# Row maxima's chain ahead of the normalisation, query rotation a quarter later, q's second component issued by ScalarE

## The reference

```python
# x: (8, 512, 256); 32 query heads in 8 groups of 4; head size 64; window 128
xn = layernorm(x)
q, k, v = xn @ Wq + bq, xn @ Wk + bk, xn @ Wv + bv       # k and v: 8 heads
q, k = rope(q) * D ** -0.25, rope(k) * D ** -0.25        # interleaved pairs (even, odd)
    # first = even * cos - odd * sin;  second = odd * cos + even * sin
scores = where(|i - j| <= 128, q @ k.T, -1e9)
probs = softmax(concat([scores, sinks]))[..., :-1]
s = (probs @ v) @ Wo + bo
g = silu(fp8_quantised(xn) @ W_ffn.T + b_ffn)
out = x + s * g
```

## Time and profile before

| | |
|---|---|
| median of 3 runs | 2094.28 us (2089.43 to 2124.69) |
| profiled execution | 2088.92 us; span of its instructions 2087.2 us |
| PE busy | 1823.7 us (87%) |
| VectorE / ScalarE / POOL busy | 1304.4 (62%) / 727.5 (35%) / 1018.1 (49%) |
| mean granted PE clock | 0.896 of full speed |
| chain that ended last | PE 54%, DMA 10%, issue 9%, POOL 8%, VectorE 6%, SyncE's queue 6%, ScalarE 3% |
| steps | one of 64 takes some 28 to 36 us |

### The profile page before, as it was taken

How to read it: one execution, slowest core, us unless ns; L and a number is a source line. 1 busy time by engine, 2 the same in 40 slices (tenths; PEclk the granted TensorE clock), 3 DMA queues, 4 the chain that set the end, 5 groups by cost and what they waited for, 6 DMA issues and landing times.

```text
span 2087.2 us, 33771 instructions
## 1 busy us (share of the span) xinstructions
PE 1823.7 (87%) x11139; PEld 1603.5 (77%) x11139; DVE 1304.4 (62%) x4156; ACT 727.5 (35%) x1509; POOL 1018.1 (49%) x1019
## 2 busy tenths in 40 slices
PE   2379999999989899989989999899998989999998
PEld 1168888888878787778878888787887878878887
DVE  7646666656756666666666666665665666665564
ACT  2123333333433333333333333333343333333332
POOL 4335445545644554564464554554454554555451
PEclk8578998989999899998899889998899988999899
DMA  4442442443354343435235244344334434234441
GB/s 156 96 82 44 87 70 52 92 72 71 53 94 71 67 77 64 78 64 92 51 68 97 49 77 70 56 87 77 57 62 84 75 71 77 51 71 75 77 74 25
DMA packets 80957, 151.92 MB, mean 73 GB/s; under 512 B 12944, under 2 KB 30096, under 8 KB 76688
## 3 DMA queue, kind: packets, MB, share of 16 engines
q1 hardware_dynamic: 80784, 149.76, 38.8%
HBM read 18.64 MB, written 4.19 MB: 11 GB/s over the span
## 4 chain that ended last, share of the span: by engine, by line
PE 54%; DMA 10%; issue 9%; POOL 8%; DVE 6%; SPq 6%; ACT 3%; DVEq 0%; POOLq 0%
PE pv_bank L1142 16%; DMA qT_full<-q_second_hi 9%; PE ring L1103 8%; PE ring L1050 7%; PE score L1126 6%; PE score L1128 6%; PE acc L1165 5%; DVE junk L858 2%; PE ring L1059 2%; PE ring L1152 2%; SPq L369 2%; SPq L381 1%; POOL stage L544 1%; DMA qT_high<-turned_rows 1%; POOL q_second L500 1%
## 5 line engine op out<-in xcount | busy, mean ns | idle before, releaser
L858 DVE CUSTOM_DVE_ANT_0 junk<-ring,mask 128x384 bf16<-128x384 f32 (+1 forms) x1024 | 488.6, 485 | 573.0 <-PE ring L1103 564.7
L1142 PEld LDWEIGHTS pv_bank<-v,stage 128*128 128x128 f32 x5120 | 741.8, 206 | 26.5 <-issue 8.2
L1142 PE MATMUL pv_bank<-v,stage 128*128 128x65 f32 x5120 | 738.5, 278 | 1.0 <-ACT stage L623 0.5
L544 POOL TENSOR_SCALAR_AFFINE_SELECT stage<-stage 128x512 f32<-128x512 f32 x384 | 251.4, 670 | 714.0 <-ACT stage L623 713.9
L1103 PE MATMUL ring<-kT_high,qT_full 128*128 128x384 f32 (+1 forms) x1024 | 411.9, 403 | 83.7 <-DVE row_max L858 45.9
L623 ACT ACTIVATE stage<-score 128x512 f32<-128x512 f32 x640 | 356.4, 594 | 367.6 <-PE score L1128 366.5
L1126 PE MATMUL score<-qT_full,kT_high 128*128 128x512 f32 x640 | 290.9, 455 | 33.2 <-ACT stage L623 15.4
L1103 PEld LDWEIGHTS ring<-kT_high,qT_full 128*128 128x128 f32 x1024 | 212.6, 208 | 133.4 <-DVE row_max L858 78.6
L1128 PE MATMUL score<-qT_high,kT_low 66*128 66x512 f32 x640 | 274.4, 429 | 0.0
L664 ACT ACTIVATE oT_hi<-ring 128x256 fp32r<-128x256 f32 x256 | 98.4, 384 | 392.4 <-PE ring L1152 392.4
L485 POOL TENSOR_TENSOR q_first<-q_even,cos 128x512 f32<-128x512 f32 x64 | 82.3, 1286 | 255.8 <-DMA qT_full<-q_second_hi 255.8
(11 more groups left out here) (118 smaller groups left out, 2770.4 us busy)
## 6 DMA issues: line engine op xcount, KB each, us to landing
qT_high<-qT_full SPq DMA_DIRECT2D x64, 512.0 KB, 4.5
qT_full<-q_first SPq DMA_DIRECT2D x64, 256.0 KB, 4.2
qT_full<-q_first_hi SPq DMA_DIRECT2D x64, 256.0 KB, 5.6
qT_full<-q_second SPq DMA_DIRECT2D x64, 256.0 KB, 6.8
qT_full<-q_second_hi SPq DMA_DIRECT2D x64, 256.0 KB, 8.0
kT_high<-k_first_hi SPq DMA_DIRECT2D x128, 64.0 KB, 2.4
kT_high<-k_second_hi SPq DMA_DIRECT2D x128, 64.0 KB, 2.2
x_res<-in_x SPq DMA_DIRECT2D x11, 512.0 KB, 8.8
```

The lines of the kernel that those rows point to most:

```text
L544: nc.gpsimd.affine_select(out=pr, in_=pr, compare_op=ALU.is_ge, fill=0.0, base=0, pattern=[[0, GROUP], [sign, P]], channel_multiplier=-sign) \
L858: nc.vector.tensor_tensor_reduce(junk[:, h % 2, 0:cols], ring[h % 2][:, 0:cols], mask[:, m0:m0 + cols], 1.0, LOWEST, ALU.add, ALU.max, row ...
L1142: last = nc.tensor.matmul(pv[:, h, :], prob[:, q % 2 * 3 + n, h * P:(h + 1) * P], v[:, slot, k, :], start=(n == 0), stop=(n == len(BLOCKS[ ...
```

## The change

SyncE keeps only the first component in `queries_in`; the new `seconds_placed` issues the second component's two transfers from ScalarE, at the end of q=3, behind the same waits. The keys of k=6 are issued last in SyncE's step. POOL's `turn_even` goes from the end of q=0 to q=1 behind the cuts, with `turn_odd` behind it; `turn_rest` and `first_low` go to q=2 and `second_low` to q=3; `keys_low` of k=2 goes from q=2 to q=0. ScalarE's `first_high` goes from q=1 to q=2, `second_high` from q=1 to q=3 (behind the exponentials) and `keys_high` of k=2 from q=1 to q=0. VectorE's `negated` runs at the end of q=0 and q=2, ahead of `normalised`, and no more at the start of q=1 and q=3; in q=3 `o_low` goes behind the last maximum. PE's last row product of q=3 goes ahead of the last weighting. No arithmetic is added or left out.

```diff
--- before.py
+++ after.py
@@ -372,15 +372,12 @@
 
             def queries_in(a):
 
-                parts = ((0, q_first, q_first_hi, s_first_lo, s_qT_first_in),
-                         (HALF, q_second, q_second_hi, s_second_lo, s_qT_second_in))
                 upto(sp, s_score_pe, NB * (a - 1))
-                for row, low, high, ready, done in parts:
-                    sp.wait_ge(ready, a + 1)
-                    upto(sp, done, Q_IN * a)
-                    sp.dma_start(qT_full[row:row + HALF, a % 2, :, :].bitcast(F32), low[:, :]).then_inc(done, 16)
-                    sp.dma_start(qT_full[D + row:D + row + HALF, a % 2, :, :].bitcast(F32), high[:, :]) \
-                        .then_inc(done, 16)
+                sp.wait_ge(s_first_lo, a + 1)
+                upto(sp, s_qT_first_in, Q_IN * a)
+                for row, part in ((0, q_first), (D, q_first_hi)):
+                    sp.dma_start(qT_full[row:row + HALF, a % 2, :, :].bitcast(F32), part[:, :]) \
+                        .then_inc(s_qT_first_in, 16)
 
             def highs_in(b):
 
@@ -412,12 +409,14 @@
                     rows_in(it, 1)
                 if k == 0 and n >= 1:
                     result(n - 1, 0)
-                if real(t) and t % QUAD == 0:
+                if real(t) and k == 2:
                     keys_in(t)
                 if real(it + 1):
                     rows_in(it + 1, 0)
                 if real(a):
                     queries_in(a)
+                if real(t) and k == 6:
+                    keys_in(t)
                 if k == 0 and n >= 1:
                     result(n - 1, 1)
                 if it == 0:
@@ -555,22 +554,22 @@
                         rstd_of((it + 2) * TILES + q + 2)
                     if (k, q) == (1, 2) and 0 <= n < BATCH - 1:
                         rstd_of(n + BATCH)
-                    if q == 1 and real(a):
-                        turn_odd(a)
-                    if q == 3 and k == 6 and new_keys:
+                    if (k, q) == (6, 3) and new_keys:
                         keys_low(quad)
                     if real(it):
                         cut(it, q)
-                    if q == 0 and real(a):
+                    if q == 1 and real(a):
                         turn_even(a)
-                    if q == 1 and real(a):
+                        turn_odd(a)
+                    if q == 2 and real(a):
                         turn_rest(a)
                         first_low(a)
-                        second_low(a)
                     if (k, q) in ((2, 0), (6, 2)) and new_keys:
                         keys_sum(quad)
-                    if (k, q) == (2, 2) and new_keys:
+                    if (k, q) == (2, 0) and new_keys:
                         keys_low(quad)
+                    if q == 3 and real(a):
+                        second_low(a)
                     if k == 0 and n >= 1 and q in (1, 3):
                         finish(n - 1, q // 2)
 
@@ -643,6 +642,15 @@
                 act.wait_ge(s_rope, 6 * a + 6)
                 nc.scalar.activation(q_second_hi[:, :].bitcast(F32R), q_second[:, :], ACT.Copy) \
                     .then_inc(s_second_hi, 1)
+
+            def seconds_placed(a):
+
+                upto(act, s_score_pe, NB * (a - 1))
+                act.wait_ge(s_second_lo, a + 1)
+                upto(act, s_qT_second_in, Q_IN * a)
+                for row, part in ((HALF, q_second), (D + HALF, q_second_hi)):
+                    nc.scalar.dma_start(qT_full[row:row + HALF, a % 2, :, :].bitcast(F32), part[:, :]) \
+                        .then_inc(s_qT_second_in, 16)
 
             def keys_high(quad):
                 act.wait_ge(s_k_summed, 2 * quad + 2)
@@ -680,6 +688,8 @@
                         exps(it, q, 1)
                     if q == 0 and real(a):
                         odd_out(a)
+                    if q == 3 and real(a):
+                        second_high(a)
                     if other is not None and other[0] == "x":
                         x_high(other[1], 0)
                         x_high(other[1], 1)
@@ -694,10 +704,11 @@
                         max_rows(b, 0)
                     if real(back(it, q, 2)[0]):
                         o_high(*back(it, q, 2))
-                    if q == 1 and real(a):
+                    if q == 2 and real(a):
                         first_high(a)
-                        second_high(a)
-                    if (k, q) in ((2, 1), (6, 2)) and quad < BATCH * QUADS:
+                    if q == 3 and real(a):
+                        seconds_placed(a)
+                    if (k, q) in ((2, 0), (6, 2)) and quad < BATCH * QUADS:
                         keys_high(quad)
                     if it < 0 and fill + FIRST_CHUNKS < N_CHUNKS:
                         chunk_high(fill + FIRST_CHUNKS)
@@ -963,10 +974,6 @@
                     fill = (it + 2) * TILES + q
                     other = chunk_at(n, k, q)
                     r, tile = back(it + 1, q, 1)
-                    if q == 1 and real(it):
-                        negated(it, 1)
-                    if q == 3 and real(b):
-                        negated(b, 0)
                     if real(r):
                         maximum(r, tile, 0)
                     if other is not None:
@@ -979,10 +986,16 @@
                             x_low(other[1], 1)
                     beside(it, n, k, q)
                     for h in heads_of(tile)[1:]:
-                        if h == GROUP - 1 and real(back(it, q, 2)[0]):
+                        if h == GROUP - 1 and q < 3 and real(back(it, q, 2)[0]):
                             o_low(*back(it, q, 2))
                         if real(r):
                             maximum(r, tile, h)
+                    if q == 0 and real(it):
+                        negated(it, 1)
+                    if q == 2 and real(b):
+                        negated(b, 0)
+                    if q == 3 and real(back(it, q, 2)[0]):
+                        o_low(*back(it, q, 2))
                     if real(back(it, q, 1)[0]):
                         normalised(*back(it, q, 1))
                     if it < 0 and fill + 2 < BATCH:
@@ -1285,8 +1298,12 @@
                         row(1)
                         weighed(2)
                     heads_turn()
-                    weighed(3)
-                    row(3)
+                    if q == 3:
+                        row(3)
+                        weighed(3)
+                    else:
+                        weighed(3)
+                        row(3)
                     if real(c3[0]):
                         out_project(*c3)
```

## The result

The changed kernel takes 2139.22 us (median of 4 runs, 2118.75 to 2146.85) against 2092.39 for the kernel before in the same comparison: ratio 1.018, 95% interval 1.013 to 1.024. It is slower, by 1.8%, where I forecast 1975. Whether that is the forecast's "slower by over 2%" (0.09) or still "within it" (0.18), the interval doesn't tell. A ratio in this document is taken over fast executions alone and need not be the quotient of the medians beside it (1.022 here); in experiment 11 two of four executions, and in experiment 2 one of ten (2636 us), are left out of it. The profiled execution took 2135.1 us. TensorE's clock went down, not up: 0.877 over the span, before 0.896.

A forecast was written before the change was run, and what follows sets the result against it. TensorE was taken as busy nearly all the time, leaving its gaps and clock to be won. Terms -77 +36 +40 -20 -14 -21 +42 -105 sum to -119: 1975 us beside the median, range 1895 to 2090.

The forecast's parts named there:

- within it: Outcome class: measured time within about 2% of no change, 2052 to 2136 us; chance 0.18.
- Part 1: Maxima's chain, moved ahead of `normalised` with POOL idle beside it, takes 0.56 us; transposition's wait goes: -77 us.
- Part 4: `row(3)` ahead of `weighed(3)` in q=3: maximum runs beside the weighting, next query projection's wait goes: -20 us.
- Part 5: k=2: `second_high` and `keys_high` no longer ahead of the scores' exponentials; the scores' wait for ScalarE goes: -14 us.
- Rival (b): Pair 0's chain collides with POOL's products in every step, delaying `normalised` and q=3's weighting: 2183 us; chance 0.10.
- Parts 2 and 3: Later `normalised` makes the weighting wait, +36 us; pair 0's chain, at the end of q=2, meets POOL's products, +40.
- Part 2: Later `normalised` gives 0.45 us new wait at the weighting in 80 quarters q=1 and q=3: +36 us.
- Part 6: k=6 keys issued last, so SyncE no longer holds rows and queries; waits of 10.7 and 13.0 shrink: -21 us.
- Part 7: SyncE's queue delays the maxima's rows; 1.5 us wait before q=2 in k=4, 5, 7, 0.7 in k=0: +42 us.
- Part 8: ScalarE issues q's second component: costed at nothing, the four transfers taking 10.0 us; ends +77 and -38.
- Part 9: TensorE's clock: shorter waits leave 60 of the 165 us lost, -105; bounds nothing won, or 145.
- Rival (a): TensorE's gaps change place and its clock stays down; parts 1 to 7 give -14: 2080 us; chance 0.19.

The follow-up runs named there:

- experiment 11: Kernel before with only POOL's rotation a quarter later, ScalarE's compute that follows it, and SyncE's keys of k=6 last: 2069.57 us, ratio 0.976.
- experiment 2: Changed kernel with all four of q's transfers issued by SyncE again, no `seconds_placed`: 2094.31 us, ratio 0.999 to the kernel before.
- experiment 12: Best version (changed kernel, rows ahead of keys, pair 0 behind `normalised`, k=2 `keys_low` in q=1) with pair 1 behind `normalised` too: 1937.58 us, ratio 0.922.
- 8: Kernel before with only q's second component issued by ScalarE (`seconds_placed` and the shorter `queries_in`): 2153.06 us, ratio 1.025.
- 1: Changed kernel with SyncE issuing `rows_in(it, 1)` ahead of the six key transfers: 1989.78 us, ratio 0.945 to the kernel before.
- 4: Changed kernel with `rows_in(it, 1)` ahead of the keys and q's second component issued by SyncE: 2009.83 us, ratio 0.957 to the kernel before.
- 6: Changed kernel with rows ahead of keys, pair 0 behind `normalised`, and k=2 `keys_low` in q=1 behind the cuts: 1902.68 us, ratio 0.906, the fastest.
- 9: Fastest version (rows ahead of keys, pair 0 behind `normalised`, k=2 `keys_low` in q=1) with all four q transfers on SyncE: 1904.55 us, ratio 0.905.
- Experiment 7: Changed kernel with eight added products in k = 3, 4, 5 ahead of the score that opens q=2: 2070.38 us, ratio 0.987 to the kernel before.
- experiment 10: Kernel before with only VectorE's chain ahead of `normalised` and TensorE's `row(3)`, `weighed(3)` exchanged in q=3: 2185.66 us, ratio 1.037.

## Why the prediction was wrong

**Right.** Part 1 in its mechanism and size: 77.3 us at the transposition are gone, the chain takes 0.57 in every step but k = 2. Part 4: the maxima held the line of the projections for 22.1 us in 65 times, TensorE and its weight load together; now for 2.0 in two. Part 5: the 15.4 us went and k = 2 is 2.4 us shorter, not 4 or more. Rival (b) didn't happen: pair 0 mostly ends 0.3 or 1.35 us into q=3, and only in k = 6 at 3.7.

**Parts 2 and 3, right in sum by luck.** 76 us were forecast, 70.8 measured at the weighting. Part 2's short wait has the size (0.37 to 0.39 in q=1, forecast 0.45) but comes in 29 quarters and not 80: some 11 us in place of 36. The collisions take the other 60 in place of 40: pair 1 in k = 2 (a wait of 2.6 each time), pair 0 in k = 6 (2.9), and pair 0 in k = 0 and 2 (0.9 to 1.1).

**Part 6, half.** The scores' 10.7 us went; the row products' 13.0 are still 11.7.

**Part 7, the right wait at half its size.** I named the score that opens q=2 and the queue, and forecast 42 us; it measured 84.1 in 39 times. Most of the shortfall stands in steps that I had left out. Those that I named (k = 4, 5, 7 and 0) have 49 us: 2.6 a time in k = 4 and 5, 1.0 in k = 0, and in k = 7 a single wait of 0.3. The other 35 stand in k = 3 (2.9 a time, the longest) and k = 1 (1.6). In k = 4 and 5 I had 1.5 for the 2.6. The term for the work of q=1 was taken from the earlier trace rows as 5.84, and 0.45 put on top. The quarter's own work is 4.99 at full clock (experiment 12), or 5.60 with the wait of part 2 in it: the quarter in the row was not free of waiting itself (0.28 us before its transposition). That is 0.7 us a step. The rest is mostly the landing: I let q land 0.14 before q=1 as in the earlier trace rows, while it landed 0.2 to 0.45 into q=1 in k = 4, and 1.9 to 2.2 into it in k = 3 (four batch elements) and k = 0 (five), there behind the slower transfers issued in k = 2 and k = 7.

**Part 8, the step that failed outright.** "Costed at nothing", with four transfers of 10.0 us. I asked how much an issue costs ScalarE and whether two queues overlap. I didn't ask what SyncE would send in the gap that it no longer spends waiting. Experiments 2 and 8 price it: 45 us on the changed kernel, 2.5% on the kernel before. Experiments 1 and 4, and 6 and 9, show that ScalarE's own time costs nothing: where the landing is off the path, ScalarE may issue without loss. By the Trainium skill (DMA: Bandwidth & Descriptors, "Issuing engines are not separate DMA queues") a second issuing engine saves only the issuing time. The runs agree: where nothing comes between, the four take 9.9 us with one issuer and with two. The 11.5 us show that the order between the two issuers is a price of its own.

**Part 9, the step that decided the sign.** I gave 105 us back for the clock and took nothing won as the worst case, though I had written that waits of 1.5 and 2.4 us may not keep it. By the granted clock and the span, the kernel before lost 217 us (2087.2 at 0.896) and the changed one 262 (2133.3 at 0.877): 45 more lost in place of 105 won, 150 us of a miss of 164. With 3.2 us of wait the clock was 0.50 through the whole next quarter, 4.9 us lost behind one wait: dearer than the wait. Experiment 7 puts some 69 us on this in k = 3 to 5. The bound should have allowed a loss, since part 7 itself put waits in k = 4 and 5 of a length that might not keep the clock. Rival (a) had the right picture, gaps that change place and a clock that stays down, but took TensorE's gaps as a sum of -14; by the rows for TensorE's matmuls that I had priced it is +44 (77.3 + 15.4 + 10.7 + 13.0 + 6.3 = 122.7 for the transposition, the scores and the row products' issue before; 84.1 + 70.8 + 11.7 = 166.6 after), and its gaps of all kinds grew by 26 between the first step and the last; the clock was free to fall further.

**What stays open.** The length of a wait alone doesn't decide what the clock does behind it. In k = 4 of the changed kernel waits of 1.9 to 3.2 us were all followed by a q=2 at 0.50 to 0.54. In k = 1 one of 1.9 was followed by 1.00 and one of 2.6 by 0.82, and in k = 5 one of 2.7 by 1.00. What else decides it, no experiment separates. Why two of SyncE's six issues take over 1 us in the step shown was not looked into either. The shares by part depend on the order in which they are undone, as each shifts where the others meet.

## What to carry to other kernels

When a wait is removed, take the next bound's slack from a quarter with no wait in it, and price the longest wait that remains rather than their sum: one of 3 us cost more in clock than in itself. Before giving a transfer to a second issuing engine, write down what the first will send in its place, and let what is needed soonest go first in a queue: exchanging two calls was worth 149 us here. Where two engines slow each other when they meet, a quarter that becomes shorter moves the later meetings, so a small speed-up can be a loss: 35 us here (experiment 12).

## What the hardware did that I had not expected

- Added products made the kernel 69 us faster (experiment 7). A wait of 3.23 us was followed by 10.7 us at clock 0.50, one of 0.86 behind busy fillers by 5.8 at 1.00. A quarter with a wait of 0.64 in it (experiment 6) kept 1.00, the same quarter with one of 1.02 (experiment 12) fell to 0.70.
- Two transfers issued by ScalarE landed behind what SyncE had issued in the meantime: 10.3 to 11.7 us for q's four in 27 of the 32 steps of k = 0, 2, 6 and 7, in place of some 9.9. Where SyncE issued nothing between, 9.9 as on one issuer: neither gain nor loss.
- The same four tiny instructions of VectorE take 0.57 us, or up to 3.7 beside POOL's products (experiment 10).
